# Ternary weights as two soft thresholds joined in PSUM, 16x16 factor folded into v, and new queue orders around the first half of the FFN

## The reference

```
def _bitlinear(x, w_latent):
    scale = clip(mean(abs(w_latent), axis=1, keepdims=True), 1e-5, None)
    tern = clip(round(w_latent / scale), -1.0, 1.0)
    return x @ (tern * scale).T
h = _bitlinear(x, w_fc) + gate * (x @ v.T @ fast_b.T @ u.T)   # w_fc 1024x256, u 1024x16, fast_b 16x16, v 16x256
r = maximum(h, 0.0)
return _bitlinear(r * r, w_proj)                              # w_proj 256x1024
```

## Time and profile before

| what | value |
|---|---|
| median of three executions | 76.26 us (76.23 to 77.61) |
| profiled execution | 76.25 us |
| its span, first to last instruction | 74.2 us |
| busy, TensorE / VectorE / ScalarE / GpSimd | 65.0 / 52.1 / 39.7 / 40.2 us |
| mean granted TensorE clock | 0.954 |

### The profile page before, as it was taken

The page is one execution under the profiler, slowest core; times in us unless marked ns, Lnnn a source line. Parts: engine busy times, 40 slices in busy tenths (PEclk is TensorE's granted clock), DMA queues, the critical chain, the costliest instruction groups (busy, mean ns, idle before and its releaser), DMA issues.

```text
span 74.2 us, 2187 instructions
## 1 busy us (share of the span) xinstructions
PE 65.0 (88%) x902; PEld 57.6 (78%) x902; DVE 52.1 (70%) x106; ACT 39.7 (54%) x82; POOL 40.2 (54%) x46
## 2 busy tenths in 40 slices
PE   4999999999999869986678799749999999999950
PEld 3787888889987859974566577449899989999940
DVE  0000049760899999999999999999598344999850
ACT  6100005646794788920059991391739989769000
POOL 7300327891482999999999990000381999800000
PEclk9999999999999999999965559999999999999999
DMA  0999999999300000000000000000000000000044
GB/s 10 297 247 325 372 399 343 390 395 390 117 0 9 0 0 0 4 0 9 9 0 0 0 0 9 0 4 0 9 0 0 0 0 0 9 0 0 0 141 141
DMA packets 3497, 6.74 MB, mean 91 GB/s; under 512 B 528, under 2 KB 1296, under 8 KB 3488
## 3 DMA queue, kind: packets, MB, share of 16 engines
q1 hardware_dynamic: 3488, 6.60, 25.4%
HBM read 6.08 MB, written 0.52 MB: 89 GB/s over the span
## 4 chain that ended last, share of the span: by engine, by line
PE 54%; DVE 39%; issue 3%; ACT 1%
PE psum L312 14%; PE psum L465 10%; PE psum L496 10%; DVE fc_tern L770 7%; PE psum L505 4%; DVE prob_n L856 4%; DVE prob_t L861 3%; PE psum L475 3%; PE psum L414 3%; DVE fc_tern L765 2%; PE psum L407 2%; PE psum L332 2%; DVE k_spread L830 2%; DVE shifted L842 2%; DVE fc_sum L751 2%
## 5 line engine op out<-in xcount | busy, mean ns | idle before, releaser
L602 ACT ACTIVATE std<-mv,eps_sb 128x1 f32<-128x1 f32 x8 | 2.3, 293 | 13.8 <-DVE mv L786 13.8
L1023 POOL TENSOR_TENSOR kqv_sb<-head_sb 128x512 f32<-128x512 f32 x4 | 4.2, 1039 | 10.2 <-ACT head_sb L725 10.2
L782 DVE TENSOR_TENSOR h<-psum,pos_sb 128x256 f32<-128x256 f32 x4 | 1.6, 412 | 9.5 <-PE psum L312 9.5
L725 ACT ACTIVATE head_sb<-psum,fc_scale 128x256 f32<-128x256 f32 x16 | 6.7, 468 | 2.7 <-PE psum L475 2.7
L465 PE MATMUL psum<-zt_hi,fc_t 128*128 128x256 f32 x32 | 8.0, 284 | 0.0
L465 PE MATMUL psum<-zt_lo,fc_t 128*128 128x256 f32 x32 | 7.8, 279 | 0.0
L496 PE MATMUL psum<-sq_hi,mlp_t 128*128 128x256 f32 x32 | 7.8, 282 | 0.0
L496 PE MATMUL psum<-sq_lo,mlp_t 128*128 128x256 f32 x32 | 7.7, 279 | 0.0
L312 PE MATMUL psum<-head_sb 128*128 128x256 f32 x24 | 6.9, 456 | 0.0
L312 PEld LDWEIGHTS psum<-head_sb 128*128 128x128 f32 x24 | 5.5, 239 | 1.3 <-DMA head_sb<-head 0.3
L465 PEld LDWEIGHTS psum<-zt_lo,fc_t 128*128 128x128 f32 x32 | 6.0, 188 | 0.0
(11 more groups left out here) (123 smaller groups left out, 186.5 us busy)
## 6 DMA issues: line engine op xcount, KB each, us to landing
head_sb<-head SPq DMA_DIRECT2D x6, 256.0 KB, 4.9
fc_sb<-w_fc SPq DMA_DIRECT2D x2, 512.0 KB, 7.7
mlp_sb<-w_mlp SPq DMA_DIRECT2D x2, 512.0 KB, 9.1
tail_sb<-tail SPq DMA_DIRECT2D x2, 384.0 KB, 6.4
out_t<-tail_sb SPq DMA_DIRECT2D x4, 128.0 KB, 1.8
pos_sb<-pos SPq DMA_DIRECT2D x1, 256.0 KB, 5.4
kqv_sb<-w_k SPq DMA_DIRECT2D x1, 256.0 KB, 6.5
kqv_sb<-w_q SPq DMA_DIRECT2D x1, 256.0 KB, 6.6
```

Source lines behind the costliest of these rows:

```text
L725: nc.scalar.activation(part[:, a, :], FCB[n][:, a * HT:(a + 1) * HT], ACT.Relu, scale=fc_scale[:, 0, m:m + 1]).then_inc(relu_ready, 1)
L1023: pool.tensor_tensor(sq[:, r, :, :], relu[:, r, :, :], relu[:, r, :, :], ALU.mult).then_inc(sq_pool, 1)
```

## The change

The two comparisons and the subtraction go. Each weight tile w now gives two independent bf16 tiles: `over` = max(w, s/2) - s/2, and `under` = min(w, -s/2) + s/2. TensorE multiplies both by the identity into the same fp32 PSUM columns, which adds and transposes them, and ScalarE writes the sign of the sum as `fc_t` or `mlp_t`. `over` is Relu(w - s/2) on ScalarE for fc tiles 2 to 7 and mlp tile 0, VectorE for fc tiles 0 and 1, GpSimd for mlp tile 1. `under` is GpSimd's for all ten tiles.

```
+            def unders(w, scale, dst, tiles, scaled, signal):          # GpSimd
+                    pool.tensor_scalar(dst[:, m, :], w[:, m, :], scale[:, 2, m:m + 1], scale[:, 1, m:m + 1],
+                                       ALU.min, ALU.add).then_inc(signal, 1)
+            def fc_overs(tiles):                                       # VectorE, tiles 0 and 1
+                    dve.tensor_scalar(fc_over[:, m, :], fc_sb[:, m, :], fc_scale[:, 1, m:m + 1],
+                                      fc_scale[:, 2, m:m + 1], ALU.max, ALU.add).then_inc(fc_over_dve, 1)
+                    nc.scalar.activation(fc_over[:, m, :], fc_sb[:, m, :], ACT.Relu,      # ScalarE, tiles 2 to 7
+                                         bias=fc_scale[:, 2, m:m + 1]).then_inc(fc_over_act, 1)
+            def turn_fc(i):                                            # turn_mlp(i) alike
+                        for n, part in enumerate((fc_over, fc_under)):
+                            mm = pe.matmul(fct_ps[i][:, k, m * P:(m + 1) * P], part[:, 4 * i + m, k * P:(k + 1) * P],
+                                           ident_bf[:, :], start=n == 0, stop=n == 1)
+            def fc_signs(i):                                           # mlp_signs(i) alike
+                nc.scalar.activation(fc_t[:, :, i * 512:(i + 1) * 512], fct_ps[i], ACT.Sign).then_inc(fct_ready, 1)
```

More of the change, by code:

```diff
@@ L463, in hidden_main @@
                     for k in range(KE):
[L464 to L467, removed]
+                        for part in parts:
+                            pe.matmul(FCB[n][:, a * HT:(a + 1) * HT], fc_t[:, k, m * P:(m + 1) * P], part[f][:, k, :],
+                                      start=a == 0 and k == 0 and part is z2t_hi, stop=False, skip_group_check=True)
             def hidden_low(f, j):
@@ L542, in _ @@
             value(1)
+            pe.wait_ge(shift_ready, 1)
+            pe.wait_ge(v_copied, 1)
+            turn_u()
             score_bias(1)
             scores(1)
-            pe.wait_ge(shift_ready, 1)
+            pe.wait_ge(ut_ready, 2)
             pe.wait_ge(q_copied, 2)
-            pe.wait_ge(v_copied, 1)
             values(0)
             pe.wait_ge(v_copied, 2)
+            pe.wait_ge(k_copied, 2)
             turn_fc(0)
             pe.wait_ge(shift_ready, 2)
-            turn_u()
+            turn_fc(1)
@@ L553, in _ @@
             pe.wait_ge(duo_ready, 3)
-            turn_fc(1)
             project(0)
+            turn_mlp(0)
             pe.wait_ge(fct_ready, 1)
-            pe.wait_ge(ut_ready, 2)
-            pe.wait_ge(k_copied, 2)
-            values(1)
[L560 to L566, removed]
+            turn_mlp(1)
@@ new lines, in _ @@
+            pe.wait_ge(mlpt_ready, 1)
+            turn(0, z, z2t_ps[0], z2_ready, z2t_turned)
+            turn(0, h2, h2t_ps[0], h2_ready, h2t_turned)
+            hidden_main(0, 0, (z2t_hi,))
+            hidden_main(0, 1, (z2t_hi,))
+            low_rank(0)
+            hidden_main(0, 0, (z2t_lo,))
+            hidden_main(0, 1, (z2t_lo,))
+            hidden_low(0, 0)
+            pe.wait_ge(fct_ready, 2)
+            pe.wait_ge(mlpt_ready, 2)
+            values(1)
+            hidden_low(0, 1)
@@ L611, in copy_out, with mlp_overs @@
                 nc.scalar.activation(dst, src, ACT.Copy).then_inc(ready, 1)
-            def fc_sums(tiles):
+            def fc_overs(tiles):
+                act.wait_ge(fc_scaled, 3)
                 for m in tiles:
[L615 to L619, removed]
+                    nc.scalar.activation(fc_over[:, m, :], fc_sb[:, m, :], ACT.Relu,
+                                         bias=fc_scale[:, 2, m:m + 1]).then_inc(fc_over_act, 1)
+            def mlp_overs():
+                act.wait_ge(mlp_scaled, 3)
+                nc.scalar.activation(mlp_over[:, 0, :], mlp_sb[:, 0, :], ACT.Relu,
+                                     bias=mlp_scale[:, 2, 0:1]).then_inc(mlp_over_act, 1)
             def mlp_sums(o):
@@ L729, in squares @@
                 act.wait_ge(relu_ready, 2 * n + 2)
-                nc.scalar.activation(sq_hi[:, n % RING, :, :], part, ACT.Square).then_inc(sq_hi_ready, 1)
+                nc.scalar.activation(sq_hi[:, n % RING, :, :], relu[:, n % PART_RING, :, :],
+                                     ACT.Square).then_inc(sq_hi_ready, 1)
             low_high(0)
+            relus(0)
             squares(0)
+            duo_rows(1)
+            relus(1)
+            relus(2)
+            squares(1)
+            squares(2)
             norm_std(2, 1, var2, std2)
             norm_std(3, 1, var2, std2)
-            copy_out(mlp_t[:, 0:4, :], mlpt_ps[0], mlpt_turned, 1, mlpt_ready)
-            squares(1)
+            relus(3)
             copy_out(z2t_hi[1][:, :, :], z2t_ps[1][:, :], z2t_turned, 2, z2t_hi_ready)
-            squares(2)
+            squares(3)
             low_high(1)
-            for n in range(3, HALVES * STEPS):
+            relus(STEPS)
+            for n in range(STEPS, HALVES * STEPS):
+                if n + 1 < HALVES * STEPS:
+                    relus(n + 1)
                 squares(n)
@@ L948, in _ @@
             normalise2(1)
-            ternary(mlp_sb, mlp_scale, mlp_tern, 0, mlp_cmp, 1, mlp_ternary)
+            softmax_divide(1, 1)
             z2t_low(0)
-            ternary(mlp_sb, mlp_scale, mlp_tern, 1, mlp_cmp, 2, mlp_ternary)
+            softmax_turn(1)
             low_low(0)
+            square(SQ_DVE[0])
+            square_low(SQ_DVE[0])
             rows_sum(1)
@@ L962, in _ @@
             tokens_copy(1)
-            for n in range(STEPS, HALVES * STEPS):
+            for n in SQ_DVE[1:]:
                 square(n)
@@ L1000, in _ @@
             weight_low(Q, q_w_hi, q_w_lo)
+            weight_low(V, v_w_hi, v_w_lo)
             bias_parts()
```

318 lines of the change are left out of this document (149 added, 169 removed).

## The result

| what | before | changed |
|---|---|---|
| median | 76.25 us (76.01 to 77.61) | 86.91 us (86.18 to 87.21) |
| profiled execution | 76.25 us | 87.06 us |
| its span | 74.2 us | 85.0 us |
| mean granted TensorE clock | 0.954 | 0.92 |

The changed kernel takes 1.140 times as long (95% interval 1.130 to 1.149): 10.7 us more, where I had forecast 3 us less and a range up to 77.7 us.

A forecast was written before the change was run, and what follows sets the result against it. Bound by VectorE's chain from about 20 to 48 us, then TensorE's FFN. FFN start 44.3 + stage 23.3 + tail 2.65 + 2.05 around it + 0.7 for a possible gap gave 73.0 us, range 71.8 to 77.7.

The forecast's parts named there:

- rival (a): Slow GpSimd, 0.93 us a tile, holds half 0's norm before the FFN: 77.6, up to 79.0 us; chance 0.20.
- step 5: The FFN stage: 23.3 us instead of 22.24, with turn_mlp out, values(1) in and three waits of 0.85 us together.
- Step 1: Up to the softmax of half 0: VectorE's added and removed work roughly cancel; first maximum at 25.1 us (+0.35).
- Step 2: Between the softmaxes: VectorE's ternary work goes, so the maximum of half 1 starts at 33.1 us, 3.4 us earlier.
- Step 3: From values(0) to project(0): project(0) starts at 38.2 instead of 41.75 us, extra transposing products hidden under duo_rows.
- rival (b): TensorE falls to the half clock, in project(0) (75.2 us) or the first FFN steps (74.7 us); chance 0.20.
- Step 4: From project(0) to the FFN: the FFN starts at 44.3 instead of 49.31 us, 5.0 us earlier.
- (c): Head-of-line waits on ScalarE delay ReLUs and so TensorE's FFN steps: +3 us, 76.0 us; chance 0.10.
- (d): Sign in another table set than Sqrt adds four ScalarE table loads: +5.1 us, 78.1 us; chance 0.02.

The follow-up runs named there:

- the run with comparisons: Changed kernel with its eleven GpSimd min/add and max/add instructions as single comparisons (weights wrong): 79.84 us, 1.050 times before.
- cheap tiles: Changed kernel with its eleven GpSimd min/add and max/add instructions replaced by multiply pairs (weights wrong): 76.29 us, 1.002 times before.

## Why the prediction was wrong, step by step

**The price of GpSimd, the step that decided.** The mechanism was written out in rival (a), with its place: `turn_mlp(0)` ahead of the turn of z2, `mlp_signs(0)` ahead of the second std. The run with comparisons shows it at the price I assumed: `mlp_over` at 44.55 us (45.5 forecast), 79.8 us (77.6 to 79.0). What failed is the term. I took 0.40 us for min and add because a multiply pair cost that, and held the comparison for the odd one and the ceiling. It measured 1.33 us per 256 elements (1.21 without company) and 3.77 per 1024, so the twenty tile-units took 21.9 us (10.6 + 7.5 + 3.8) and not 8. The ceiling had no reason: an instruction with one operation says nothing of the most that one with two can cost. With 0.31 us more a unit for the second operation (1.24 - 0.93, times twenty: 6.2) rival (a) would have read 83.8 to 85.2 us, and the sentence "it decides from 0.9 us a tile" should have stood at its head. My range ended at 77.7 because it took in no more than the lower edge of (a). What (a) at the right price still lacks to 86.9 us is mostly step 5, an FFN 2.0 us longer than I summed.

**Step 1** was about right: the maximum of half 0 came at 25.85 us with cheap tiles and 26.28 in the changed kernel, 25.1 forecast. The two instructions of `key_spread` took 2.34 us together beside GpSimd, one of them 1.50, where I had 1.32 for both the earlier trace rows, and they and the sums stand in front.

**Step 2** rested on GpSimd being through with three tiles and two spreads at 30.7 us. It was 34.55, and the maximum of half 1 came at 37.0 instead of 33.1. With cheap tiles it came at 34.0, so here 3.0 us are GpSimd's price and 0.9 are mine.

**Step 3** kept a gap of 1.36 us inside the narrow products; it was 1.75 with cheap tiles and 0.81 in the changed kernel. No releaser is shown in any of them, and my reason, the narrow products, was wrong: it goes by the place in TensorE's list. It stands behind the engine's 468th product in the kernel before, the changed one and all eight variants. With the 14 idle products ahead it comes 14 narrow products sooner (92 of the 128 behind it, 78 without them):

```profile
34.91 1.12 PE L391 MATMUL psum<-prob_t,v_sb 32*32 32x64 f32 x92 [1.04 <-issue]
```

In each of these kernels a transfer of 16 KB on the DMA queue that the page calls "instruction" starts 0.4 to 1.8 us before the gap and lands 1.2 to 1.4 us before its end (in the kernel before 33.65 to 34.57, the gap ends at 35.96). So TensorE most likely waits there for its own instructions; no run tested that.

Then I hid 32 transposing products under `duo_rows`. The window above shows why not: the clock was at 0.54, 1.2 GHz for nearly all of it, and most of them took 0.107 us each, so the two `turn_fc` lasted 3.1 us, until 40.6, past `yt` at 40.02. project(0) started at 40.6, 38.2 forecast. That is rival (b) in another place than I had put it. Where the clock stayed up, `yt` beside GpSimd was what came last. Two causes, each enough to hide the other's cure, so neither alone is worth its length.

**Step 4** holds in its length. From project(0) to the FFN 6.1 us were forecast (38.2 to 44.3) and 6.0 measured with cheap tiles (40.60 to 46.59).

**Step 5** was too small by 2.0 us. `values(1)` in and `turn_mlp` out, +1.48 - 0.91, was right. The waits were not: by the starts of TensorE's products some 1.2 us in all before and 3.8 with cheap tiles, so about +2.6 where I had +0.45. z of half 1 costs 0.96 of them, the copy 0.5, the low part 0.2, the last squares 0.36; the rest is in pieces. The 0.7 us that I added for a second gap did not come: `values(1)` ran in 1.47 us without one, and by the reading of step 3 there was no reason for it behind these products. So the miss with cheap tiles, 3.3 us, is 2.3 of a later start and 2.0 of a longer FFN, less this 0.7; the rest, 0.3, is what its profiled execution (76.67) took more than its median. I had priced z at the 0.41 us of the earlier trace rows; here it took 1.17. VectorE and GpSimd in the changed kernel:

```profile
68.03 1.17 DVE L807 TENSOR_SCALAR z<-h,mv,rstd 128x256 f32<-128x256 f32 x1
```
```profile
67.69 1.36 POOL L1046 TENSOR_TENSOR sq_lo<-kqv_sb,sq_hi 128x512 fp32r<-128x512 f32 x1
```

Two moves against these waits (the square, in two kernels, and the early product step) each removed the one it aimed at and brought another of nearly its length. So I read the stage as held by the late norm of half 1 as a whole, project(1) behind hidden(0,3), and not by one of its instructions. That is not shown: an order with an earlier norm was not tried, nor both moves together.

**The balance of the idea.** Without the dear price the new order starts the FFN 2.7 us earlier (49.31 to 46.6) and runs it 3.1 us longer: nothing is left, and that is what 76.3 against 76.25 us says. My sum had the first at 5.0 and the second at 1.1.

**The other rivals.** (c) did not show: with cheap tiles no wait of TensorE for a ReLU stands among its waits. (d) is out: the changed kernel has three table loads, as the kernel before, at 0.71, 22.99 and 42.76 us, with Sign used between two stds.

## What to carry to other kernels

A bound has to be a bound: the nearest row limits a price only if the unknown instruction does no more than it. Where a queue holds twenty units of one unmeasured instruction and other engines' lists put the critical step behind its last one, measure it alone first. Where a gap has no releaser, count the instructions ahead of it in several kernels before pricing it by the work around it. When several waits of about the same length stand side by side, freeing one shows the next; what a new order brings is read from the stage's length, not from the wait removed.

## What the runs showed of the hardware

- GpSimd's time for a one-input `tensor_scalar` goes by the operations: per 128x256 0.42 us for two multiplications by immediates, 0.94 for one min, add or comparison, 1.24 for min/add, max/add or add/add; per 128x1024 1.08 for two multiplications and 3.81 for min/add.
- VectorE and GpSimd slow each other on operands in SBUF, but not always: z 0.41 to 1.17 us and `yt` 0.69 to 1.67 beside two-input instructions of GpSimd, `yt` 2.41 beside its multiply pairs, and GpSimd's min/add from 1.22 to 2.15 and more beside VectorE. In the changed kernel z at 46.23 took 0.41 and `yt` at 41.73 took 0.69 beside a min/add. What decides was not settled.
- The fall to 1.2 GHz near 37 us came in the profiled execution of one kernel and not in that of nearly the same one, with no product added; the mean clocks of one kernel's nine executions lie between 0.976 and 1.0.
- A gap of 0.5 to 1.9 us stands behind TensorE's 468th product in all ten kernels, and ends 1.2 to 1.4 us after a transfer of 16 KB on the instruction queue has landed.
